# Neighbour tables as one stream of slots with masked steps, and TensorE sums four rows of each step of the last attention

## The chip, the cores and the metric

One Trainium2 chip, one core. The metric is the device time of one execution in microseconds, the median of three: 5052.19 us before the change (5048.85 to 5056.97).

## The reference, cut to what matters

A network of four graph layers and four expert layers on 3125 nodes of 256 features. Two of its layers are attentions over in-edges with a softmax per target node: the gate of layer 1 (65536 edges of which those with both ends among the nodes count, 4 heads of 4 features) and the last graph layer (100000 edges, 8 heads of 32 features). The last one, which the change touches most:

```python
def _L3_gnn_ref(x, edge_index, W, att_src, att_dst, bias):
    h = jnp.einsum('nf,fhd->nhd', x, W)
    a_src = jnp.sum(h * att_src, axis=-1)
    a_dst = jnp.sum(h * att_dst, axis=-1)
    e = jax.nn.leaky_relu(a_src[src] + a_dst[dst], NEG_SLOPE)
    e_max = jax.ops.segment_max(e, dst, num_segments=N)
    e_exp = jnp.exp(e - e_max[dst])
    denom = jax.ops.segment_sum(e_exp, dst, num_segments=N)
    alpha = e_exp / (denom[dst] + 1e-16)
    msg = h[src] * alpha[:, :, None]
    out = jax.ops.segment_sum(msg, dst, num_segments=N)
    out = out.reshape(N, -1) + bias
    return jax.nn.relu(out)
```

It is followed by eight gelu experts of which each node takes two.

## The kernel before

**Tiles and stages.** The nodes are sorted by in-degree and lie in 25 tiles of 128, one node per partition; a tile needs as many slots as its largest in-degree. These are for the main graph 55, 42, 40, 39, 38, 37, 36, 35, 34, 34, 33, 32, 32, 31, 31, 30, 30, 29, 28, 28, 27, 26, 25, 23, 20 (together 815), for the gate's graph 28, 19, 17, 16, 16, 15, 15, 14, 14, 13, 13, 13, 12, 12, 11, 11, 11, 10, 10, 9, 9, 9, 8, 7, 5. The stages follow one another: "graphs" builds the tables of neighbours, "count" and the following ones (l0p, l0a, l0f, l0e) do layer 0, l1a is the gate's attention beside the experts of layer 1, l2a and l2e are layer 2, l3p prepares the rows and l3a is the last attention beside its experts.

**The tables.** In build_graphs, `fill` (L638) has VectorE lay out each tile's neighbours in the tile `ell`, 64 slots a node, and SyncE (even tiles, L338) and ScalarE's queue (odd ones, L261) write them to HBM by `write_tile` (L234): a block of 128 x 8 numbers for the main graph, 128 x 4 for the gate's, one DMA each (L239). Each tile starts at a block of its own, so its slots are rounded up: 112 blocks of 8, 92 blocks of 4. The values of empty slots (8191) are outside of the rows and gather nothing. `steps_of` (L680) plans for the gate's graph how many blocks of a tile are taken alone and how many in pairs. VectorE's last work in the stage is to place the weights of layer 2 (L3103).

**The last attention** (attend_heads_beside_experts, L2228). One step takes 8 slots. SyncE loads their indices into one of four buffers (L2338 to L2339), POOL gathers 8 rows of 264 numbers each with one indirect DMA per slot (L2355), waiting first that VectorE is done with the buffer, and VectorE does the rest in `edges` (L2508): scores (L2514), a refill of the buffer's scores with -1e30 for gathers that will skip slots (L2515), leaky relu (L2516), running maximum (L2517), difference (L2518), and a copy (L2520); ScalarE does the exp into PSUM (L2379). Before VectorE waits for that it runs `add_sums` (L2533) for the previous step's rows: 8 weighted rows to 4, 2, 1 and onto the accumulator (L2536 to L2539). After the wait it scales the accumulator (L2526), copies the weights as a 33rd column (L2527) and multiplies the 8 rows with them (L2528). A tile is an opening step, half of the pieces of expert work that fall to this tile (`at(0)`), the later steps in a loop, the other half (`at(1)`), the closing sums, and the division.

**The order of the work** is written out by hand in `tiles` (L2277): every engine runs through the same list, four tiles of attention to each group of four tiles of expert work, two pieces a tile. In one piece TensorE makes one expert's products (L2449) and the one before's outputs (L2459), ScalarE the gelus (L2393), and VectorE adds an earlier expert's output onto x (L2638). TensorE has nothing to do with the attention's steps, and after the last tile it runs the rest of the last group's experts.

**The gate's attention** (attend_beside_experts, L2660) is built alike, with rows of 24 numbers and buffers of two units of 4 slots; a step takes one unit or two, and VectorE works on each unit by its own instruction (L2936, L2949). Five registers are loaded for each tile. Between tiles stand the pieces of layer 1's experts (L2780, L2791). There are 34 steps of one unit and 29 of two.

`ch(...)` issues an instruction and waits for its end; `ch.add(...)` issues without waiting, and `ch.join()` waits for all of them.

## Time and profile before

| | us |
|---|---|
| median of three | 5052.19 |
| the profiled execution | 5050.65 |
| its span | 5049.0 |
| PE busy | 2837.1 |
| DVE (VectorE) busy | 3175.9 |
| ACT (ScalarE) busy | 1613.8 |
| POOL (GpSimd) busy | 2036.4 |

The mean granted TensorE clock is 0.83 of 2.4 GHz. The busy times don't add up to the span, since the engines work beside each other; no engine is busy throughout, so what bounds the kernel differs by stage and has to be read from stretches and waits.

### The profile page before, as it was taken

The page shows a single profiled execution, that of the slowest core. Times are in us where ns is not written, and L with a number is a line of the kernel's source. Part 1 is how long each engine was busy: PE and PEld are TensorE (multiplying, and loading weights), DVE is VectorE, ACT ScalarE, POOL GpSimd, SP SyncE. Part 2 cuts the span into 40 slices and gives each one's busy share as a digit, 9 for nine tenths or more (in the row PEclk, how much of TensorE's full clock was granted, in tenths as well). Part 3 has the DMA queues.
Part 4 walks back from the last instruction along what each step waited for, and adds up shares of the span by engine and source line. Part 5 has one row for each costly group of instructions (what it writes and reads, how often), then busy time and mean ns, then how long its engine had stood idle before and what let it go on. Part 6 is the DMA issues. An engine that isn't in the chain of part 4 may idle for free. (4 is left out here: it accounts for less than half of the span.)

```text
span 5049.0 us, 66259 instructions
## 1 busy us (share of the span) xinstructions
PE 2837.1 (56%) x15435; PEld 2098.0 (42%) x15474; DVE 3175.9 (63%) x7737; ACT 1613.8 (32%) x2880; POOL 2036.4 (40%) x1967
## 2 busy tenths in 40 slices
PE   0541055699799596467761699859400133344447
PEld 0431055587687485355551244447300122222224
DVE  8886687677577656334436754452456777777774
ACT  0243043476476121144430454322201222222222
POOL 1136410200100152577761100016377777777771
PEclk9999999899899598588885899979755566667679
DMA  0412345542442323211114554522343333333220
GB/s 33 77 20 45 17 167 196 170 139 83 166 140 83 116 65 115 91 30 35 35 38 132 196 174 161 172 91 67 101 117 91 90 90 85 93 95 84 77 63 19
DMA packets 341260, 487.28 MB, mean 97 GB/s; under 512 B 171624, under 2 KB 259056, under 8 KB 339059
## 3 DMA queue, kind: packets, MB, share of 16 engines
q1 hardware_dynamic: 204434, 259.76, 16.5%
q0 software_dynamic: 86064, 176.05, 13.2%
q10 hardware_dynamic: 50608, 49.90, 3.0%
q14 instruction: 116, 0.94, 0.1%
q8 instruction: 38, 0.62, 0.1%
HBM read 369.96 MB, written 137.24 MB: 100 GB/s over the span
## 5 line engine op out<-in xcount | busy, mean ns | idle before, releaser
L2355 POOL DMA_INDIRECT l3a_got<-rows,l3a_idx x896 | 949.4, 1060 | 304.1 <-issue 273.6
L2449 PE MATMUL ps<-l3a_xt,l3a_w 128*128 128x512 f32 (+1 forms) x448 | 266.9, 759 | 633.1 <-ACT l3a_h L2393 633.1
L1662 PE MATMUL ps<-l0a_all_rows,l0a_w 128*128 128x257 f32 x2500 | 556.8, 382 | 28.3 <-DVE l0a_w L1782 28.3
L1662 PEld LDWEIGHTS ps<-l0a_all_rows,l0a_w 128*128 128x128 f32 x2500 | 476.0, 191 | 101.9 <-issue 32.0
L2757 POOL DMA_INDIRECT l1a_got<-rows,l1a_idx x384 | 383.6, 999 | 131.3 <-issue 127.4
L2449 PEld LDWEIGHTS ps<-l3a_xt,l3a_w 128*128 128x128 f32 x448 | 112.3, 277 | 766.9 <-issue 766.6
L2077 PE MATMUL ps<-l2a_table,l2a_count 128*128 128x512 bf16 x1837 | 404.8, 380 | 40.5 <-ACT l2a_count L2002 38.6
L2379 ACT ACT_TABLE_LOAD x99 | 127.0, 1283 | 772.0 <-DVEq L2519 772.0
L2780 PE MATMUL ps<-xt,l1w_w 128*128 x640 | 208.0, 485 | 156.5 <-ACT l1a_h L2836 111.4
L2077 PEld LDWEIGHTS ps<-l2a_table,l2a_count 128*128 128x128 bf16 x1875 | 183.4, 98 | 262.1 <-issue 43.2
L1587 ACT ACTIVATE l0a_low<-ps,l0a_factors x650 | 254.6, 510 | 85.7 <-PE ps L1652 78.2
L2528 DVE TENSOR_TENSOR l3a_v<-l3a_got,ps 128x2048 f32<-128x2048 f32 x112 | 255.0, 2276 | 0.0
L3338 POOL DMA_INDIRECT l0e_xin<-routed,l0e_taking x60 | 64.0, 1067 | 450.5 <-DVEq L3534 424.0
L2459 PE MATMUL ps<-l3a_w,l3a_h 128*128 128x256 f32 x800 | 199.8, 405 | 81.5 <-DVEq L2641 79.8
L2780 PEld LDWEIGHTS ps<-xt,l1w_w 128*128 128x128 f32 x640 | 135.2, 214 | 225.9 <-issue 181.6
L2459 PEld LDWEIGHTS ps<-l3a_w,l3a_h 128*128 128x128 f32 x800 | 160.9, 204 | 129.4 <-issue 108.1
L1166 POOL DMA_INDIRECT rows<-own_rows,node x50 | 48.9, 977 | 403.8 <-DVEq L1034 394.0
L1782 DVE TENSOR_TENSOR l0a_w<-l0a_w,l0a_held 128x1280 f32<-128x1280 f32 x130 | 192.7, 1484 | 13.2 <-DVE xt L1817 13.2
L2791 PE MATMUL ps<-l1w_w,l1a_h 128*128 128x256 f32 x800 | 180.5, 385 | 29.9 <-ACT l1a_h L2836 29.9
L2791 PEld LDWEIGHTS ps<-l1w_w,l1a_h 128*128 128x128 f32 x800 | 154.5, 194 | 52.6 <-issue 31.0
L1973 POOL DMA_DIRECT2D l2a_seen<-l2a_state x13 | 9.2, 704 | 410.6 <-DMA l2a_state<-l2a_seen 385.7
L1768 DVE TENSOR_TENSOR l0a_w<-l0a_w,l0a_low 128x1280 f32<-128x1280 f32 x78 | 116.4, 1493 | 82.2 <-ACT l0a_w L1593 71.9
(995 smaller groups left out, 6622.9 us busy)
## 6 DMA issues: line engine op xcount, KB each, us to landing
l0a_held<-counts SPq DMA_DIRECT2D x130, 640.0 KB, 3.9
counts<-count_held SPq DMA_DIRECT2D x13, 3200.0 KB, 9.9
l2a_held<-counts SPq DMA_DIRECT2D x65, 640.0 KB, 4.0
l3a_got<-rows,l3a_idx POOLq DMA_INDIRECT x896, 2.8
l_y<-l1a_y_sb ACTq DMA_DIRECT2D x20, 640.0 KB, 3.4
l2a_table<-rows SPq DMA_DIRECT2D x16, 640.0 KB, 7.5
l2a_state<-l1a_fresh ACTq DMA_DIRECT2D x1, 9984.0 KB
l2a_seen<-l2a_state POOLq DMA_DIRECT2D x12, 768.0 KB, 5.9
```

What stands on the lines that cost most here:

```text
L1587: ins = act.activation(low_at(n * Q + q, h), spread_of(n, W, 2 * W), ACT.Copy, scale=factors[:, C, at:at + 1])
L1662: ins = pe.matmul(sums_of(n, k, D + 1), w[:, at, k * P:(k + 1) * P], all_rows[:, at, 1:RW], start=(at == 0), stop=False)
L1782: dve.tensor_tensor(chunk(q), chunk(q), held_of(n, q), ALU.mult).then_inc(weighed, 1)
L2077: ins = pe.matmul(bank_of(b, g, k).rearrange("p o n -> p (o n)"), count[:, at, k * P:(k + 1) * P], table[:, part, at, :], start=(at == 0 a ...
L2355: pool.indirect_dma_start(out=got[:, at:at + RW], out_offset=None, in_=rows[:, :], in_offset=bass.IndirectOffsetOnAxis(ap=idx[:, a, k:k + ...
L2379: act.activation(p, d[:, :, :], ACT.Exp).then_inc(exped, 1)
L2449: ins = pe.matmul(ps[:, m, 0:size * P], w1[:, x, k, m * P:(m + 1) * P], xt[:, 0:size, k, :], start=(k == 0), stop=(k == KT - 1))
L2459: ins = pe.matmul(ps[:, 2 + j // 2, (j % 2) * D:(j % 2 + 1) * D], h[:, x % 2, m, j * P:(j + 1) * P], w2[:, x, m, :], start=(m == 0), stop= ...
L2528: ch.add(dve.tensor_tensor(rows_v[:, :, :, 0:DH], buffer(b)[:, :, 0:D].rearrange("p s (h d) -> p s h d", h=H), p[:, 0:SLOTS, :].unsqueeze( ...
L2757: pool.indirect_dma_start(out=got[:, at:at + RW], out_offset=None, in_=rows[:, :], in_offset=bass.IndirectOffsetOnAxis(ap=idx[:, a, k:k + ...
L2780: ins = pe.matmul(ps[:, 2 * (m % 2) + q, 0:(hi - lo) * P], w1[:, x, k, m * P:(m + 1) * P], xt[:, bass.ds(i * C + lo, hi - lo), k, :], star ...
L2791: ins = pe.matmul(ps[:, 4 + j // 2, (j % 2) * D:(j % 2 + 1) * D], h[:, m, j * P:(j + 1) * P], w2[:, x, m, :], start=(m == 0 and j % 2 == 0 ...
```

## The change

The tables become [128, columns], one stream of slots: each tile gets as many slots as its largest in-degree (at least 8), and the next tile's follow at once. A step still takes 8 slots that begin at a multiple of 8, so that a tile can share its first and its last octet with its neighbours; a mask of -1e30 is added to the scores of the slots that belong to others. Empty slots point to a row behind the last node's, which SyncE writes before the gathers, so buffers are not refilled. SyncE and ScalarE's queue write only full octets of a tile, wait for all of them, and then write one closing octet per tile that may overlap the one before. In the last attention VectorE adds four of the eight weighted rows onto the others, and TensorE sums the four into a PSUM bank with products with the identity; VectorE adds this onto the accumulator one step later. The counting stage fetches a tile's slots as one run per partition. In l2a a constant and a shift change with the table's unit.

The diff, cut to its core:

```diff
-UNIT = 4
+FEWEST = SLOTS
...
-def write_tile(eng, s, t, stored):
-    n_units = eng.value_load(s.trips_i[0:1, bass.ds(t, 1)], min_val=1, max_val=s.whole_row)
-    to = eng.value_load(s.dest_i[0:1, bass.ds(t, 1)], min_val=0, max_val=s.blocks - s.whole_row)
-    with eng.Fori(0, n_units) as u:
-        eng.dma_start(s.table[bass.ds((to + u) * (P * s.slots), P * s.slots), 0].rearrange("(p s) -> p s", s=s.slots),
-                      s.ell[:, bass.ds(t, 1), bass.ds(u * s.slots, s.slots)].rearrange("p o s -> p (o s)")).then_inc(stored, 16)
+def write_table(eng, s, odd, emptied=None):
+    eng.wait_ge(s.sized, 1)
+    n = eng.value_load(s.chunk_i[0:1, 0:1], min_val=1, max_val=s.chunks)
+    with eng.Fori(0, n) as k:
+        for half, (lo, hi) in enumerate(s.halves):
+            when(eng, c, s.filled, k * 2 + (half + 1))
+            with eng.Fori((lo + 1 - odd) // 2, (hi + 1 - odd) // 2) as h:
+                t = h * 2 + odd
+                n_units = eng.value_load(s.trips_i[0:1, bass.ds(t, 1)], min_val=1, max_val=s.whole_row)
+                to = eng.value_load(s.dest_i[0:1, bass.ds(t, 1)], min_val=0, max_val=s.columns - WIDE)
+                with eng.Fori(0, n_units) as u:
+                    eng.dma_start(s.table[:, bass.ds(to + u * SLOTS, SLOTS)],
+                                  s.ell[:, bass.ds(t, 1), bass.ds(SLOTS + u * SLOTS, SLOTS)].rearrange("p o s -> p (o s)")).then_inc(s.stored, 16)
+        done = eng.value_load(s.wrote_i[0:1, 0:1], min_val=1, max_val=s.chunks * NT * s.whole_row)
+        when(eng, c, s.stored, done * 16)
+        with eng.Fori(0, (NT + 1 - odd) // 2) as h:
+            t = h * 2 + odd
+            at = eng.value_load(s.last_i[0:1, 0, bass.ds(t, 1)], min_val=1, max_val=WIDE)
+            to = eng.value_load(s.last_i[0:1, 1, bass.ds(t, 1)], min_val=0, max_val=s.columns - WIDE)
+            eng.dma_start(s.table[:, bass.ds(to, SLOTS)],
+                          s.ell[:, bass.ds(t, 1), bass.ds(at, SLOTS)].rearrange("p o s -> p (o s)")).then_inc(s.closed, 16)
+        if emptied is not None:
+            when(eng, c, s.closed, k * (16 * NT) + 16 * NT)
+            eng.sem_inc(emptied, 1)
...
+def whole_table(s):
+    write_table(sp, s, 0, s.emptied)
+    total = sp.value_load(s.base_row[0:1, NT:NT + 1], min_val=1, max_val=s.trash - 2 * WIDE)
     for k in range(2):
-        sp.dma_start(s.table[bass.ds((total + k * s.whole_row) * (P * s.slots), P * WIDE), 0].rearrange("(p s) -> p s", s=WIDE),
-                     empty[:, :]).then_inc(s.padded, 16)
-even_tiles(m)
-even_tiles(g)
+        sp.dma_start(s.table[:, bass.ds(total + k * WIDE, WIDE)], empty[:, :]).then_inc(s.padded, 16)
+whole_table(m)
+whole_table(g)
...
-ch(dve.tensor_scalar(units[:, 0:NT], row[:, 0:NT], float(s.slots * (s.least - 1) + 1), float(s.slots - 1), ALU.max, ALU.add))
-ch(dve.tensor_copy(row_i[:, 0:NT], units[:, 0:NT]))
-ch(dve.tensor_scalar(row_i[:, 0:NT], row_i[:, 0:NT], s.slots.bit_length() - 1, None, ALU.logical_shift_right))
-ch(dve.tensor_copy(units[:, 0:NT], row_i[:, 0:NT]))
+ch(dve.tensor_scalar(units[:, 0:NT], row[:, 0:NT], float(FEWEST), None, ALU.max))
...
-m.ch.add(dve.memset(empty[:, :], NOBODY))
+m.ch.add(dve.memset(empty[:, :], c.N))
...
-steps_of(g, True)
...
-b = eng.value_load(base_row[0:1, bass.ds(i * 2 + par, 1)], min_val=0, max_val=blocks - 2 * UNITS)
-at = (b + k * UNITS) % units
-eng.dma_start(tile[:, par, :].rearrange("p (u s) -> p u s", s=SLOTS),
-              table[bass.ds(at * (P * SLOTS), P * WIDE), 0].rearrange("(u p s) -> p u s", p=P, s=SLOTS)).then_inc(landed, 16)
+b = eng.value_load(base_row[0:1, bass.ds(i * 2 + par, 1)], min_val=0, max_val=columns - 2 * WIDE)
+at = (b + k * WIDE) % total
+eng.dma_start(tile[:, par, :], table[:, bass.ds(at, WIDE)]).then_inc(landed, 16)
...
+class Stream:
+    def __init__(self, c, table, base_row):
+        self.base_row, self.columns = base_row, table.shape[1]
+        self.table, self.NT = table, c.NT
+    def total(self, eng):
+        return eng.value_load(self.base_row[0:1, self.NT:self.NT + 1], min_val=1, max_val=self.columns - 4 * WIDE)
+    def rounds(self, total):
+        return (total + RING * SLOTS) // (RING * SLOTS)
+    def octet(self, o):
+        return self.table[:, bass.ds(o * SLOTS, SLOTS)]
+    def bounds(self, eng, t):
+        begins = eng.value_load(self.base_row[0:1, bass.ds(t, 1)], min_val=0, max_val=self.columns - 4 * WIDE)
+        ends = eng.value_load(self.base_row[0:1, bass.ds(t + 1, 1)], min_val=FEWEST, max_val=self.columns - 4 * WIDE)
+        return begins, ends
+def fill_masks(dve, ch, c, masks):
+    row = c.iota[:, 0:SLOTS].unsqueeze(2).broadcast_to([P, SLOTS, SLOTS])
+    slot = c.iota[:, 0:SLOTS].unsqueeze(1).broadcast_to([P, SLOTS, SLOTS])
+    ch.add(dve.tensor_tensor(masks[:, 0, :, :], slot, row, ALU.is_lt))
+    ch.add(dve.tensor_tensor(masks[:, 1, :, :], slot, row, ALU.is_ge))
+    ch.add(dve.memset(masks[:, 2, :, :], 0.0))
+    ch.join()
+    ch(dve.tensor_scalar(masks[:, 0:2, :, :], masks[:, 0:2, :, :], FLOOR, None, ALU.mult))
+def mask_of(masks, row, H):
+    return masks[:, :, :, :].rearrange("p k r j -> p (k r j)")[:, bass.ds(row * SLOTS, SLOTS)].unsqueeze(2).broadcast_to([P, SLOTS, H])
+def closing_row(ends, o):
+    return SLOTS + ends % SLOTS + (ends // SLOTS - o + 65535) // 65536 * SLOTS
...
+weighed_rows = lambda o: rows_v[:, bass.ds(o % 2, 1), :, :, :].rearrange("p o s h d -> p (o s) h d")
+totals = ps[:, 6, 0:VW]
...
+sp.wait_ge(blank, 2)
+sp.dma_start(rows[c.N:c.N + 1, :], nobody[:, :]).then_inc(blank_in, 16)
...
-total = pool.value_load(base_row[0:1, c.NT:c.NT + 1], min_val=1, max_val=blocks - 2 * RING)
-last_node = pool.to_reg(c.N - 1)
-with pool.Fori(0, (total + (RING - 1)) // RING) as q:
+rounds = stream.rounds(stream.total(pool))
+last_node, last_row = pool.to_reg(c.N - 1), pool.to_reg(c.N)
+pool.wait_ge(blank_in, 16)
+with pool.Fori(0, rounds) as q:
     for a in range(RING):
         when(pool, c, idx_in[a], (q + 1) * 16)
-        when(pool, c, valued, q * (2 * RING) + (2 * a + 2))
+        when(pool, c, freed, q * RING + (a + 1))
...
+def sums(t, o):
+    when(pe, c, valued, o + t + 1)
+    rows_now = weighed_rows(o)
+    for k in range(ADDED):
+        ins = pe.matmul(totals, c.ident[:, :], rows_now[:, k, :, :].rearrange("p h d -> p (h d)"),
+                        start=(k == 0), stop=(k == ADDED - 1))
+    ins.then_inc(summed, 1)
+def tile(t, begins, ends, at):
+    sums(t, begins // SLOTS)
     at(0)
+    with pe.Fori(begins // SLOTS + 1, ends // SLOTS + 1) as o:
+        sums(t, o)
...
-    ch(dve.memset(buffer(a), FLOOR))
-    dve.sem_inc(valued, 2)
+dve.memset(nobody[:, 0:D], 0.0).then_inc(blank, 1)
+dve.memset(nobody[:, D:RW], FLOOR).then_inc(blank, 1)
+dve.sem_inc(freed, RING)
+fill_masks(dve, ch, c, masks)
...
-def edges(t, b, opening):
+def edges(t, o, row, opening):
     ch.restart()
-    when(dve, c, arrived, b + 1)
-    scores = buffer(b)[:, :, D:RW]
+    when(dve, c, arrived, o + 1)
+    rows_now = weighed_rows(o)
     er = c.er[:, bass.ds(t * 8, H)].unsqueeze(1).broadcast_to([P, SLOTS, H])
-    ch(dve.tensor_tensor(e[:, 0:SLOTS, :], scores, er, ALU.add))
-    ch.add(dve.tensor_scalar(scores, e[:, 0:SLOTS, :], 0.0, FLOOR, ALU.mult, ALU.add))
+    ch(dve.tensor_tensor(e[:, 0:SLOTS, :], buffer(o)[:, :, D:RW], er, ALU.add))
+    ch(dve.tensor_tensor(e[:, 0:SLOTS, :], e[:, 0:SLOTS, :], mask_of(masks, row, H), ALU.add))
     ch(dve.scalar_tensor_tensor(e[:, 0:SLOTS, :], e[:, 0:SLOTS, :], SLOPE, e[:, 0:SLOTS, :], ALU.mult, ALU.max))
     ch(dve.tensor_reduce(top[:, :], e[:, :, :].rearrange("p s h -> p h s"), AX, ALU.max))
     ch(dve.tensor_tensor(d[:, :, :], e[:, :, :], top[:, :].unsqueeze(1).broadcast_to([P, SLOTS + 1, H]), ALU.subtract))
     dve.sem_inc(shifted, 1)
     ch.add(dve.tensor_copy(e[:, SLOTS, :], top[:, :]))
-    if not opening:
-        add_sums()
     dve.wait_ge(exped, 1)
     dve.sem_clear(exped)
-    ch.add(dve.tensor_tensor(acc[:, :, :], acc[:, :, :], spread(p[:, SLOTS, :], DH + 1), ALU.mult))
-    ch.add(dve.tensor_copy(rows_v[:, :, :, DH], p[:, 0:SLOTS, :]))
-    ch.add(dve.tensor_tensor(rows_v[:, :, :, 0:DH], buffer(b)[:, :, 0:D].rearrange("p s (h d) -> p s h d", h=H),
+    ch.add(dve.tensor_copy(rows_now[:, :, :, DH], p[:, 0:SLOTS, :]))
+    ch.add(dve.tensor_tensor(rows_now[:, :, :, 0:DH], buffer(o)[:, :, 0:D].rearrange("p s (h d) -> p s h d", h=H),
                              p[:, 0:SLOTS, :].unsqueeze(3).broadcast_to([P, SLOTS, H, DH]), ALU.mult))
     ch.join()
-    dve.sem_inc(valued, 2)
-def add_sums():
-    rows = rows_v
-    ch(dve.tensor_tensor(rows[:, 0:4, :, :], rows[:, 0:4, :, :], rows[:, 4:8, :, :], ALU.add))
-    ch(dve.tensor_tensor(rows[:, 0:2, :, :], rows[:, 0:2, :, :], rows[:, 2:4, :, :], ALU.add))
-    ch(dve.tensor_tensor(rows[:, 0, :, :], rows[:, 0, :, :], rows[:, 1, :, :], ALU.add))
-    ch(dve.tensor_tensor(acc[:, :, :], rows[:, 0, :, :], acc[:, :, :], ALU.add))
-def tile(t, b0, b1, at):
+    ch(dve.tensor_tensor(rows_now[:, 0:ADDED, :, :], rows_now[:, 0:ADDED, :, :], rows_now[:, ADDED:SLOTS, :, :], ALU.add))
+    if not opening:
+        add_sums(o + t)
+        ch(dve.tensor_tensor(acc[:, :, :], acc[:, :, :], spread(p[:, SLOTS, :], DH + 1), ALU.mult))
+    dve.sem_inc(valued, 1)
+def add_sums(done):
+    when(dve, c, summed, done)
+    ch(dve.tensor_tensor(acc[:, :, :], by_head(totals), acc[:, :, :], ALU.add))
+def tile(t, begins, ends, at):
     ch.restart()
     ch.add(dve.memset(e[:, SLOTS, :], START))
     ch.add(dve.memset(acc[:, :, :], 0.0))
     ch.join()
-    edges(t, b0, True)
+    edges(t, begins // SLOTS, begins % SLOTS, True)
     at(0)
-    with dve.Fori(b0 + 1, b1) as b:
-        edges(t, b, False)
+    with dve.Fori(begins // SLOTS + 1, ends // SLOTS + 1) as o:
+        dve.sem_inc(freed, 1)
+        edges(t, o, closing_row(ends, o), False)
     ch.restart()
     at(1)
-    add_sums()
+    add_sums(ends // SLOTS + t + 1)
...
-def bounds_of(eng, t):
-    b0 = eng.value_load(step_rows[0:1, 0, bass.ds(t, 1)], min_val=0, max_val=blocks)
-    alone = eng.value_load(step_rows[0:1, 1, bass.ds(t, 1)], min_val=1, max_val=2)
-    pairs = eng.value_load(step_rows[0:1, 2, bass.ds(t, 1)], min_val=1, max_val=blocks)
-    return b0, alone, pairs
...
-when(pool, c, freed, q * (2 * RING) + (2 * a + 2))
+when(pool, c, freed, q * RING + (a + 1))
...
-def edges(b, unit, lo):
+def edges(o, row):
     ch.restart()
-    parts = [(unit + h, lo + h * UNIT) for h in range((SLOTS - lo) // UNIT)]
-    here, through, last = slice(lo, SLOTS), slice(lo, SLOTS + 1), len(parts)
-    when(dve, c, arrived, unit + last)
-    er = er_of.broadcast_to([P, UNIT, H])
-    for u, at in parts:
-        ch.add(dve.tensor_tensor(e[:, at:at + UNIT, :], buffer(u, VW, VW + H), er, ALU.add))
-    ch.join()
-    for u, at in parts:
-        ch.add(dve.tensor_scalar(buffer(u, VW, VW + H), er, 0.0, FLOOR, ALU.mult, ALU.add))
-    ch(dve.scalar_tensor_tensor(e[:, here, :], e[:, here, :], SLOPE, e[:, here, :], ALU.mult, ALU.max))
-    ch(dve.tensor_reduce(top[:, :], e[:, through, :].rearrange("p s h -> p h s"), AX, ALU.max))
-    ch(dve.tensor_tensor(d[:, through, :], e[:, through, :], top[:, :].unsqueeze(1).broadcast_to([P, SLOTS + 1 - lo, H]), ALU.subtract))
+    when(dve, c, arrived, o + 1)
+    ch(dve.tensor_tensor(e[:, 0:SLOTS, :], buffer(o, VW, VW + H), er_of.broadcast_to([P, SLOTS, H]), ALU.add))
+    ch(dve.tensor_tensor(e[:, 0:SLOTS, :], e[:, 0:SLOTS, :], mask_of(masks, row, H), ALU.add))
+    ch(dve.scalar_tensor_tensor(e[:, 0:SLOTS, :], e[:, 0:SLOTS, :], SLOPE, e[:, 0:SLOTS, :], ALU.mult, ALU.max))
+    ch(dve.tensor_reduce(top[:, :], e[:, :, :].rearrange("p s h -> p h s"), AX, ALU.max))
+    ch(dve.tensor_tensor(d[:, :, :], e[:, :, :], top[:, :].unsqueeze(1).broadcast_to([P, SLOTS + 1, H]), ALU.subtract))
     dve.sem_inc(shifted, 1)
     ch(dve.tensor_copy(e[:, SLOTS, :], top[:, :]))
     dve.wait_ge(weighed, 1)
     dve.sem_clear(weighed)
-    for u, at in parts:
-        ch.add(dve.tensor_tensor(
-            v[:, at:at + UNIT, :].rearrange("p s (h d) -> p s h d", h=H),
-            buffer(u, 0, VW).rearrange("p s (h d) -> p s h d", h=H),
-            p[:, at:at + UNIT, :].unsqueeze(3).broadcast_to([P, UNIT, H, DH]), ALU.mult))
+    ch.add(dve.tensor_tensor(v[:, :, :].rearrange("p s (h d) -> p s h d", h=H),
+                             buffer(o, 0, VW).rearrange("p s (h d) -> p s h d", h=H),
+                             p[:, 0:SLOTS, :].unsqueeze(3).broadcast_to([P, SLOTS, H, DH]), ALU.mult))
     ch.add(dve.tensor_tensor(by_head(acc), by_head(acc), spread(p[:, SLOTS, :]), ALU.mult))
     ch.join()
-    dve.sem_inc(freed, last)
     ch.add(dve.tensor_tensor(p[:, SLOTS, :], p[:, SLOTS, :], den, ALU.mult))
-    ch.add(dve.tensor_reduce(part[:, :], v[:, here, :].rearrange("p s w -> p w s"), AX, ALU.add))
+    ch.add(dve.tensor_reduce(part[:, :], v[:, :, :].rearrange("p s w -> p w s"), AX, ALU.add))
     ch.join()
-    ch.add(dve.tensor_reduce(den, p[:, through, :].rearrange("p s h -> p h s"), AX, ALU.add))
+    ch.add(dve.tensor_reduce(den, p[:, :, :].rearrange("p s h -> p h s"), AX, ALU.add))
     ch.add(dve.tensor_tensor(acc, acc, part[:, :], ALU.add))
     ch.join()
-b0, alone, pairs = bounds_of(dve, t)
-u0 = dve.value_load(base_row[0:1, bass.ds(t, 1)], min_val=0, max_val=blocks)
-u1 = dve.value_load(step_rows[0:1, 3, bass.ds(t, 1)], min_val=1, max_val=blocks)
-with dve.Fori(0, alone) as i:
-    edges(b0 + i, u0 + i, UNIT)
+begins, ends = stream.bounds(dve, t)
+edges(begins // SLOTS, begins % SLOTS)
 beside()
-with dve.Fori(0, pairs) as i:
-    edges(b0 + alone + i, u1 + i * 2, 0)
+with dve.Fori(begins // SLOTS + 1, ends // SLOTS + 1) as o:
+    dve.sem_inc(freed, 1)
+    edges(o, closing_row(ends, o))
```

## Rows read from the trace of the kernel before

**Rows 1.** Gathers of both attentions; first and last step of l3a.
```profile
L2355 POOL DMA_INDIRECT l3a_got<-rows,l3a_idx x896 | 949.4, 1060 | 304.1 <-issue 273.6
...
L2757 POOL DMA_INDIRECT l1a_got<-rows,l1a_idx x384 | 383.6, 999 | 131.3 <-issue 127.4
...
L2514 DVE TENSOR_TENSOR l3a_e<-l3a_got,er x112: 224/226/269, 3691.0 to 4932.8; 128x64 f32 x64, 128x64 f32<-128x64 f32 x48
```

**Rows 2.** Busy time by stretches: span, PE, PEld, DVE, ACT, POOL, PEclk, DMA share, GB/s.
```profile
3690.00:3790.00 100.00, 0.00 (x0) 0.00 (x0) 69.65 (x143) 7.03 (x15) 77.76 (x74) 0.50 0.33 84
...
4800.00:4900.00 100.00, 40.34 (x124) 25.14 (x124) 76.83 (x175) 23.54 (x31) 69.52 (x66) 0.73 0.25 64
```

**Rows 3.** Waits of stage l3a: total us, times, longest.
```profile
DVE l3a_e L2514 <- SPq L2338: 87.1, 27, 16.2
...
POOL l3a_got L2355 <- DVEq L2531: 22.8, 8, 5.4
```

**Rows 4.** VectorE in order of time: start, length, operation, [idle before].
```profile
4598.71 0.22 DVE L2514 TENSOR_TENSOR l3a_e<-l3a_got,er 128x64 f32 x1 [0.59 <-DVE l3a_acc L2544]
...
4600.14 0.17 DVE L2520 COPY l3a_e<-l3a_top 128x8 f32<-128x8 f32 x1
...
4601.81 0.43 DVE L2526 TENSOR_TENSOR l3a_acc<-l3a_acc,ps 128x264 f32<-128x264 f32 x1 [1.50 <-ACT ps L2379]
...
4605.17 1.66 DVE L2638 SCALAR_TENSOR_TENSOR x<-ps,l3a_g_now,x 128x256 f32 x4 [0.60 <-DVE l3a_v L2528]
...
4618.11 0.23 DVE L2514 TENSOR_TENSOR l3a_e<-l3a_got,er 128x64 f32 x1 [0.94 <-DVE l3a_v L2528]
...
4618.37 0.19 DVE L2515 TENSOR_SCALAR l3a_got<-l3a_e 128x64 f32 x1
...
4618.48 0.22 DVE L2516 SCALAR_TENSOR_TENSOR l3a_e<-l3a_e 128x64 f32<-128x64 f32 x1
...
4619.43 0.17 DVE L2520 COPY l3a_e<-l3a_top 128x8 f32<-128x8 f32 x1
...
4622.57 0.43 DVE L2526 TENSOR_TENSOR l3a_acc<-l3a_acc,ps 128x264 f32<-128x264 f32 x1
...
4626.25 0.23 DVE L2514 TENSOR_TENSOR l3a_e<-l3a_got,er 128x64 f32 x1 [0.92 <-DVE l3a_v L2528]
```

**Rows 5.** ScalarE, TensorE in order of time; then the table loads of l3a.
```profile
4600.15 1.28 ACT L2379 ACT_TABLE_LOAD   x1 [17.88 <-DVEq L2519]
...
4601.44 0.23 ACT L2379 ACTIVATE ps<-l3a_d 128x72 f32<-128x72 f32 x1
...
4603.82 5.15 PE L2449 MATMUL ps<-l3a_xt,l3a_w 128*128 128x512 f32 x8 [11.76 <-ACT l3a_h L2393]
...
4608.81 3.62 PE L2459 MATMUL ps<-l3a_w,l3a_h 128*128 128x256 f32 x16
...
L2379 ACT ACT_TABLE_LOAD x99 | 127.0, 1283 | 772.0 <-DVEq L2519 772.0
```

**Rows 6.** Busy time by stretches of l1a, columns as in rows 2.
```profile
2300.00:2400.00 100.00, 73.03 (x275) 55.81 (x276) 40.73 (x219) 39.97 (x63) 76.53 (x78) 0.85 0.17 35
...
2500.00:2600.00 100.00, 87.43 (x355) 67.43 (x354) 39.87 (x207) 45.87 (x72) 75.95 (x77) 0.95 0.18 39
```

**Rows 7.** VectorE by line, 4300 to 4957: busy us, mean ns | idle before.
```profile
L2536 DVE TENSOR_TENSOR l3a_v<-l3a_v 128x1056 f32<-128x1056 f32 x56 | 70.2, 1254 | 1.9
```

**Rows 8.** Waits of stage l1a.
```profile
DVE l1a_e L2936 <- DMA l0a_held<-counts: 91.2, 21, 5.0
```

**Rows 9.** SyncE's queue and VectorE at the end of the graphs stage.
```profile
466.31 79.27 SPq L239 DMA_DIRECT2D table_main<-graphs_main_ell  x59
...
556.01 0.88 SPq L351 DMA_DIRECT2D table_main<-graphs_empty  x2
...
559.58 66.92 SPq L239 DMA_DIRECT2D table_gate<-graphs_five  x49
...
634.73 1.89 DVE L3103 COPY_PREDICATED wt<-graphs_set_mask,graphs_set_w_now 128x256 f32<-128x256 int32 x4
```

245 lines of the change are left out of this document (108 added, 137 removed).

## The prediction

> **What bounds the kernel now.** I read the busy table by stretches first, then the waits, then single steps in order of time. The steps of the last attention (stage l3a) run from 3691.0 to 4932.8 us on VectorE [rows 1]. Early on POOL is busy 77.8 us of 100 and VectorE 69.7; near the end POOL has fallen to 69.5 and VectorE risen to 76.8 [rows 2]. One gather of the gate attention takes 1.00 us busy with 0.33 us of issue around it [rows 1], and those here mostly the same, so 77% is about all that POOL can show: the first part goes by gathers, and the later part by VectorE. The waits agree: VectorE waits 87.1 us for gathered octets, POOL only 22.8 us for freed buffers [rows 3]. So VectorE has 87 us of slack in the whole stage; whatever it gains or loses beyond that is the stage's time, since the TensorE tail starts from its last tile.
>
> A later step of VectorE takes 8.14 us, 4618.11 to 4626.25 [rows 4]. Of these the exp wait is fully hidden: ACT's exp needs a 1.28 us table load and 0.23 us [rows 5], and in that time VectorE does the four sums of the step before, 3.14 us from the copy (4619.43) to the scaling (4622.57). The opening step has no sums to do and shows the bare wait: copy 4600.14, scaling 4601.81, 1.67 us with 1.50 of it idle for ACT; it takes 6.46 us up to the work after it at 4605.17 [rows 4]. The gate attention (l1a) is bound by gathers: POOL 76 to 77% busy in every stretch [rows 6], and of its 131.3 us idle all but 3.9 is issue [rows 1].
>
> **The change, part by part.** *Counts.* From the in-degrees of the 25 tiles (55, 42, 40, ... 20; sum 815 slots), the main table had 112 octets, so 112 steps and 896 gathers. As a stream it has 815 slots, 104 octets with the last round, 832 gathers; but a tile that begins and ends inside octets touches more of them: 126 steps, 25 opening and 101 later ones instead of 87. The gate table (321 slots) goes from 384 to 352 gathers, and from 63 steps (34 of half width) to 65 of full width.
>
> *A later step of l3a.* From 8.14: take out the stretch of the sums, -3.14, and put in the bare exp wait, +1.67. The refill of the buffer goes, -0.11 (4618.37 to 4618.48, where the next operation begins beside it). A mask add of the size of the first add comes in, chained, +0.26 (4618.11 to 4618.37). The scaling of the accumulator leaves its old place, -0.35, and stands at the end behind a chain, +0.46. The first of the old adds, 1056 elements, 1.254 us [rows 7], stays but no longer covers anything, +1.28 with its gap. Adding TensorE's totals from PSUM, 264 elements: +0.55 with the wait. Sum 8.76 us. *Opening step:* 6.46 - 0.11 + 0.26 - 0.35 + 1.28 = 7.54. *Closing:* the four sums, 3.0 us, become one add, 0.55. Together: 101 x 8.76 - 87 x 8.14 = +177; 25 x 1.08 = +27; -25 x 2.45 = -61. That is **+142 us** of VectorE's own time: fewer elements per step, but more steps, and the cover of exp gone.
>
> *Registers.* The mask's row, the octet's parity and two buffer addresses are computed by VectorE's sequencer. Part runs under the operation before. Nothing shows this arithmetic; bounds 0 (all hidden) and 0.7 us a step (nearly the 0.92 us by which 4626.25 follows one step's product [rows 4], again), 0 to +88; I take 0.2 us, **+25**, since most of it can be done before the operation it waits for ends.
>
> *Waiting for TensorE.* Each step gives TensorE four fp32 products with the identity, 264 columns, 8 records. The 16 records of 256 columns took 3.62 us [rows 5], so 1.87 us at that pace. TensorE will have been idle for some microseconds before; where it is idle the granted clock is 0.50 [rows 2], the 1.2 GHz level, so twice that, 3.7 us. In later steps it is hidden (the totals are wanted a whole step later). At a tile's close the experts' adds take 1.7 to 1.9 us, 4605.17 for four [rows 4], and the rest shows: 25 x 1.8 = **+45** (0 at the 2.4 GHz level).
>
> *Slack.* VectorE's 87.1 us of waiting for octets goes, since POOL now needs 832 x 1.31 = 1090 us, the 1.31 being 1.00 / 0.767 [rows 6], against VectorE's nearly 1400: **-87** (-60 if part of it is the first tiles waiting behind SP's weight loads). POOL's waits for freed buffers grow instead and cost nothing.
>
> So l3a: +142 + 25 + 45 - 87 = **+125**.
>
> *Gate attention.* 32 gathers fewer at 1.33 us [rows 1] is -42. VectorE loses three of five register loads per tile (the 91.2 us idle before its first add, 21 times 4.3 us [rows 8], labelled with a DMA it doesn't wait for), and gains a mask add and wider steps; it has room, being about 40% busy. In the late tiles TensorE is 87% busy [rows 6] and keeps the pace, so part is lost there: **-35** (-50 to -25). POOL's wait for SP's write of the empty row is 2 to 3 us at the start, within this.
>
> *Building the tables.* SP writes 59 units of the main table in 79.3 us and 49 of the gate's in 66.9 [rows 9], and ACT the rest beside it. It now writes only full units (90 of 112, and about 31 of 92, over both queues), then waits for all to land (10.4 us passed from the last issue to the pad at 556.01; with fewer writes I take 7 to landing), then writes one closing octet per tile, 13 on SP at about 2.3 us with their two register loads (a fit to the two SP rows: 1.0 us within a tile, 2.55 across). Main: 536, landed 543, closed 575. Gate: full ones by 614, closed by 647, padded by 652. VectorE's last placing ends at 636.6 [rows 9], and this is what ends the stage now: **+15** (0 to +35). The step plan that goes (2.6 us) and the small operations that come into the fill cancel.
>
> The counting's fetch of one run of 256 bytes a partition in place of eight short ones: the fetches run a pair of tiles ahead of their use, and only the first, one short transfer, is waited for; 0. Changes in l2a are one constant and a shift; 0.
>
> **Sum:** +125 - 35 + 15 = +105 on the profiled execution's own 5050.65 us (span 5049.0), which is 1.5 below the median of the three: **5155 us**.
>
> **A rule against the trace.** The exp begins at 4601.44 where the load of 4600.15 ends: a switch costs 1.28 us, and the bare wait is 1.50 [rows 4, 5]. The Trainium skill ("ScalarE: Activation LUTs", "What ACT_TABLE_LOAD costs") adds a drain of about 1.38 us to each switch; the trace has none in this chain. If it showed up once the wait is exposed, 126 steps would lose about 174 us more, an estimate from that page's figure, and the time would be about 5330.
>
> **Rivals.** (1) *Gathers stay the bound, faster.* l3a would shrink by 64 x 1.33 = 85, l1a by 42, building +15: 4939 us. For it: POOL at 77% [rows 2]. Against: it holds only while VectorE needs less than 10.5 us per gathered octet, and I get (1242 - 87 + 212) / 104, 13.1: the stage's steps without their waits, and what is added. 0.05. (2) *Exp without its table load.* 99 of the 112 exps had one; without them 126 x 1.28 = 161 less: 4994. For it: in most later steps exp follows exp, with no other function between. Against: if all 25 opening steps have a load, 74 of the 87 later ones have one too [rows 5], so they are loaded again regardless. 0.04. (3) *Hidden after all.* Registers, closing wait and building at 0: 142 - 87 - 35 = +20, 5071. 0.12. (4) *TensorE in lockstep is late.* Behind each opening step it has an expert turn, 5.15 + 3.62 us [rows 5], before the next step's sums; at the 1.2 GHz level about 17 us against VectorE's 18.6 until it needs them. If it misses by 3 us a tile, +75: 5230. 0.08. (5) The drain, 5330: 0.02. (6) The counts aren't what I say: 0.01, any side. The forecast keeps 0.68.
>
> **Numbers.** A measurement of this kernel tells about 0.2% (10 us) from no change. Forecast with its bounds (registers -25 to +63, closing wait -45 to 0, slack 0 to +27, building -15 to +20, l1a -15 to +10), not all at one end: 5095 to 5210; the range reaches down to rival 3 and up to rival 4. Faster: rivals 1, 2 and a tail of 3, 0.10. Same: 0.06. Slower: 0.84.
>
> **What would show it.** Right: 126 scores, 832 and 352 gathers; after the copy of each later step VectorE idle about 1.5 us for ACT; later steps 8.9 to 9.0 us apart; POOL's idle put down to VectorE freeing buffers; VectorE no longer waiting for SP; the counting stage begun at about 652. Wrong: a later step under 8.3 us, exp without its load, POOL still 77% busy throughout, or VectorE waiting for TensorE's sums inside a tile.

## The result, and the profile after

The changed kernel takes 5318.77 us (5317.60 to 5319.46, 4 runs) against 5053.5 of the kernel before in the same comparison: a ratio of 1.0525, 95% interval 1.0507 to 1.0544. It is slower, as forecast, but by 265 us where 105 were forecast, and outside of the range of 5070 to 5230. The profiled execution took 5319.1 us, 268.5 more than that of before.

Lines of the page after: the span, the busy times, the granted clock by slices, and the costliest groups that answer to those of before.

```profile
span 5317.5 us, 69508 instructions
...
PE 3201.6 (60%) x16481; PEld 2369.6 (45%) x16482; DVE 3158.9 (59%) x7592; ACT 1635.9 (31%) x2910; POOL 1951.8 (37%) x1871
...
PEclk9999999899997896798858998896666677677778
...
L2384 POOL DMA_INDIRECT l3a_got<-rows,l3a_idx x832 | 909.6, 1093 | 607.7 <-DVEq L2587 350.4
...
L2455 PE MATMUL ps<-l3a_v,ident 128*128 x1008 | 446.2, 618 | 767.8 <-DVEq L2573 767.8
...
L2408 ACT ACT_TABLE_LOAD x112 | 143.7, 1283 | 970.8 <-DVEq L2560 970.8
```

The counts are those of the forecast: 832 gathers, 126 steps (1008 records of TensorE's sums are 126 times 8). VectorE's busy time fell, from 3175.9 to 3158.9 us, while the kernel grew by 5%: the time is not in the operations but between them. The stretches of the last attention, early and late, in the columns of [rows 2]:

```profile
3710.00:3810.00 100.00, 34.23 (x72) 22.59 (x72) 59.04 (x114) 6.39 (x14) 77.73 (x74) 0.59 0.46 100
4800.00:4900.00 100.00, 56.90 (x168) 39.51 (x168) 62.82 (x134) 21.14 (x28) 60.31 (x55) 0.72 0.27 73
```

POOL begins at its 77% and ends at 60, and VectorE is at 63% where it was at 77: nobody is busy, so something waits. The waits of the stage (total us, times, longest):

```profile
DVE l3a_v L2565 <- ACT ps L2408: 192.5, 125, 2.0
...
DVE l3a_e L2556 <- DVE l3a_e L2555: 67.5, 126, 0.7
...
DVE l3a_e L2555 <- SPq L2366: 29.6, 4, 18.2
...
DVE l3a_acc L2578 <- PE ps L2455: 22.9, 11, 4.4
...
POOL l3a_got L2384 <- DVEq L2587: 350.4, 23, 21.2
```

VectorE stands 192.5 us for the exp (34.3 in the 24 opening steps before), and 67.5 us between its first two operations. Its wait for gathers fell from 87.1 [rows 3] to 29.6 us, and POOL now waits 350.4 us for VectorE to free buffers. Where the waits lie in a step is seen in order of time (start, length, operation, [idle before]); this is the later step that answers to the 8.14 us of [rows 4]:

```profile
4702.30 0.23 DVE L2555 TENSOR_TENSOR l3a_e<-l3a_got,er 128x64 f32 x1 [0.98 <-DVE l3a_acc L2572]
...
4703.13 0.23 DVE L2556 TENSOR_TENSOR l3a_e<-l3a_e,l3a_masks 128x64 f32<-128x64 f32 x1 [0.60 <-DVE l3a_e L2555]
...
4704.37 0.17 DVE L2561 COPY l3a_e<-l3a_top 128x8 f32<-128x8 f32 x1
...
4706.21 0.27 DVE L2565 COPY l3a_v<-ps 128x64 f32 x1 [1.67 <-ACT ps L2408]
...
4706.37 2.29 DVE L2566 TENSOR_TENSOR l3a_v<-l3a_got,ps 128x2048 f32 x1
...
4708.82 1.26 DVE L2569 TENSOR_TENSOR l3a_v<-l3a_v  x1 [0.16 <-DVE l3a_v L2566]
...
4710.32 0.43 DVE L2578 TENSOR_TENSOR l3a_acc<-ps,l3a_acc 128x264 f32<-128x264 f32 x1 [0.24 <-DVE l3a_v L2569]
...
4710.78 0.43 DVE L2572 TENSOR_TENSOR l3a_acc<-l3a_acc,ps 128x264 f32<-128x264 f32 x1
...
4712.18 0.22 DVE L2555 TENSOR_TENSOR l3a_e<-l3a_got,er 128x64 f32 x1 [0.97 <-DVE l3a_acc L2572]
```

From 4702.30 to 4712.18 it takes 9.88 us. ScalarE in the same step:

```profile
4704.38 1.28 ACT L2408 ACT_TABLE_LOAD   x1 [8.37 <-DVEq L2560]
4705.68 0.23 ACT L2408 ACTIVATE ps<-l3a_d 128x72 f32<-128x72 f32 x1
```

Between the first add (L2555) and the mask (L2556) VectorE stands 0.60 us. The view by line gives what its queue does there; under it are the same two operations in an opening step, whose mask row is `begins % SLOTS` and needs less arithmetic than `closing_row`:

```profile
L2556 DVEq FUSED_REGOPS  x227: 113/176/322, 3711.4 to 5195.7; - x114
...
4730.51 0.23 DVE L2555 TENSOR_TENSOR l3a_e<-l3a_got,er 128x64 f32 x1 [0.67 <-DVE l3a_acc L2583]
...
4730.93 0.23 DVE L2556 TENSOR_TENSOR l3a_e<-l3a_e,l3a_masks 128x64 f32<-128x64 f32 x1 [0.20 <-DVE l3a_e L2555]
```

FUSED_REGOPS are register operations (count, then shortest, median and longest in ns). In the later step above they run from 4702.56 to 4703.08: they begin 0.04 us after the first add has ended, and so they do in the other steps (median of 126). `ch(...)` has VectorE's queue wait for the end of an operation before it takes the next thing in the program, and the arithmetic stands behind that wait. Nothing covers it.

The time of the whole, by the first and last operation of the stages on VectorE, in the profiled executions: the counting begins at 654.8 instead of 638.4 us (+16.4); the stages up to the gate's attention add 5.4; the gate's attention with what waits for it, from its first operation to the gate's own, takes 556.7 instead of 560.5 (-3.8); up to the first score of the last attention +2.1; from the first to the last step's score there 1484.0 instead of 1241.8 (+242.2); the rest +6.2. Sum +268.5.

### The profile page after: what moved, and what is told of

Read it like the earlier page. It is cut to its first block and busy times, and to the rows that moved or that the text cites. A ratio compares the mean times of both kernels' runs of the same rounds, so it can differ in the third digit from the quotient of the medians.

```text
span 5317.5 us, 69508 instructions
## 1 busy us (share of the span) xinstructions
PE 3201.6 (60%) x16481; PEld 2369.6 (45%) x16482; DVE 3158.9 (59%) x7592; ACT 1635.9 (31%) x2910; POOL 1951.8 (37%) x1871
## 5 line engine op out<-in xcount | busy, mean ns | idle before, releaser
L2384 POOL DMA_INDIRECT l3a_got<-rows,l3a_idx x832 | 909.6, 1093 | 607.7 <-DVEq L2587 350.4
L2455 PE MATMUL ps<-l3a_v,ident 128*128 x1008 | 446.2, 618 | 767.8 <-DVEq L2573 767.8
L2455 PEld LDWEIGHTS ps<-l3a_v,ident 128*128 128x128 f32 x1008 | 297.4, 309 | 904.2 <-issue 834.1
L2794 POOL DMA_INDIRECT l1a_got<-rows,l1a_idx x352 | 351.1, 997 | 158.7 <-issue 117.4
L2566 DVE TENSOR_TENSOR l3a_v<-l3a_got,ps 128x2048 f32 x126 | 288.4, 2289 | 1.0 <-issue 1.0
L2489 PE MATMUL ps<-l3a_xt,l3a_w 128*128 128x512 f32 (+1 forms) x448 | 200.7, 596 | 8.6 <-ACT l3a_h L2422 8.5
L2499 PE MATMUL ps<-l3a_w,l3a_h 128*128 128x256 f32 x800 | 187.4, 387 | 3.5 <-DVEq L2681 3.5
L2569 DVE TENSOR_TENSOR l3a_v<-l3a_v x126 | 158.6, 1259 | 19.8 <-DVE l3a_v L2566 19.8
```

Of the source, the lines that this page charges most:

```text
L2384: pool.indirect_dma_start(out=got[:, at:at + RW], out_offset=None, in_=rows[:, :], in_offset=bass.IndirectOffsetOnAxis(ap=idx[:, a, k:k + ...
L2455: ins = pe.matmul(totals, c.ident[:, :], rows_now[:, k, :, :].rearrange("p h d -> p (h d)"), start=(k == 0), stop=(k == ADDED - 1))
L2489: ins = pe.matmul(ps[:, m, 0:size * P], w1[:, x, k, m * P:(m + 1) * P], xt[:, 0:size, k, :], start=(k == 0), stop=(k == KT - 1))
L2499: ins = pe.matmul(ps[:, 2 + j // 2, (j % 2) * D:(j % 2 + 1) * D], h[:, x % 2, m, j * P:(j + 1) * P], w2[:, x, m, :], start=(m == 0), stop= ...
L2566: ch.add(dve.tensor_tensor(rows_now[:, :, :, 0:DH], buffer(o)[:, :, 0:D].rearrange("p s (h d) -> p s h d", h=H), p[:, 0:SLOTS, :].unsqueez ...
L2569: ch(dve.tensor_tensor(rows_now[:, 0:ADDED, :, :], rows_now[:, 0:ADDED, :, :], rows_now[:, ADDED:SLOTS, :, :], ALU.add))
```

## Experiments

The theory I tested: VectorE's own chain of dependent operations sets the last attention, and the step grew by the bare wait for the exp, by the mask, and by register arithmetic between the operations. The rivals: TensorE in lockstep sets the pace; or the stream's additional steps alone cost nearly everything. The kernel before took 5051 to 5056 us beside all runs but three, which are named. The diffs are in the last attention, unless it says otherwise.

**blocks_pe_sums: TensorE's sums alone, with the tables of before.**

```diff
-                    if not opening:
-                        add_sums()
                     dve.wait_ge(exped, 1)
...
                     dve.sem_inc(valued, 2)
+                    halve(b)
+                    if not opening:
+                        add_sums(b)
+                        ch(dve.tensor_tensor(acc[:, :, :], acc[:, :, :], spread(p[:, SLOTS, :], DH + 1), ALU.mult))
+                    dve.sem_inc(halved, 1)
```

> The kernel before with its tables as they are, and only the sums of the last attention moved: VectorE adds four of eight rows after the product, TensorE sums the four. The chain theory (VectorE's own chain of dependent operations with the bare exp wait in it sets l3a): a later step goes from 8.14 to about 9.2 us, the closing sums shrink; own time +70 us, of which the 87 us in which VectorE waited for gathers take in a part: 5065 to 5125 us, likeliest 5090. The rival that TensorE's products are what is waited for: most of the change's 265 us is here too, 5200 or more.

Measured 5098.87 us, ratio 1.0086 (1.0056 to 1.0115). A later step takes 9.10 us (median), 0.96 more than before. The two waits that tell it:

```profile
DVE l3a_v L2539 <- ACT ps L2382: 169.1, 111, 2.0
...
DVE l3a_e L2529 <- SPq L2341: 43.2, 13, 16.6
```

The exp's wait is there in all steps, and half of VectorE's 87.1 us of waiting for gathers has been used up to pay for it. So moving the sums costs 43 us by itself.

**stream_own_sums: the stream and its masks alone,** with the sums back on VectorE in the exp wait.

```diff
                     ch.add(dve.tensor_copy(e[:, SLOTS, :], top[:, :]))
+                    if not opening:
+                        add_sums()
                     dve.wait_ge(exped, 1)
...
-                    ch(dve.tensor_tensor(rows_now[:, 0:ADDED, :, :], rows_now[:, 0:ADDED, :, :], rows_now[:, ADDED:SLOTS, :, :], ALU.add))
-                    if not opening:
-                        add_sums(o + t)
```

> The changed kernel with its stream of slots and its masks, but with the sums of the last attention done by VectorE in the exp wait, as before. The chain theory: a later step at 8.9 to 9.1 us (8.14, less the refill, plus 0.83 for the mask and its row), 101 of them: 5200 to 5230 us. If the 14 more steps and the mask cost little: under 5120.

Measured 5220.26 us, ratio 1.0326 (1.0296 to 1.0356); a later step 8.84 us, slightly under what was expected, the whole inside. The stream is the larger part, +164 us; it and the sums make 207 of the 265. Most of the missing 58 is slack that can be spent only once: of VectorE's 87.1 us of waiting for gathers 43.2 are left in blocks_pe_sums, 31.3 here and 29.6 in the change, so the two halves took 43.9 and 55.8 and the whole only 57.5, which is 42 less. Another 13 are 14 more steps with the 0.96 us of blocks_pe_sums.

**middle_unmasked: masks only on a tile's first and last octet.**

```diff
-                    with dve.Fori(begins // SLOTS + 1, ends // SLOTS + 1) as o:
+                    with dve.Fori(begins // SLOTS + 1, ends // SLOTS) as o:
                         dve.sem_inc(freed, 1)
-                        edges(t, o, closing_row(ends, o), False)
+                        edges(t, o, None, False)
+                    dve.sem_inc(freed, 1)
+                    edges(t, ends // SLOTS, ends % SLOTS + SLOTS, False)
```

> The changed kernel, with the loop over later steps ended one octet earlier and without mask, and the closing octet written out behind it with its mask; the result is the same, since only a tile's first and last octet hold slots of others. The chain theory: 76 of 101 later steps lose the mask add and the arithmetic on its row, 0.83 us each, and the closing one some of the arithmetic: -63 to -75 us, 5244 to 5256. If the row's arithmetic is hidden or something else bounds the steps: less than -30 us.

Measured 5249.92 us, ratio to before 1.0384 (1.0354 to 1.0415), 69 us under the change. An operation of 0.23 us and the register arithmetic for its row in each of the 76 middle steps, 0.91 us a step, cost a quarter of the whole loss, and they are not needed there: only first and last octets hold slots of other tiles.

**one_product: one of TensorE's four products in each step** (three of the four rows are left out of the sums).

```diff
-                    for k in range(ADDED):
+                    for k in range(1):
```

> The changed kernel, but TensorE forms only one of the four products of each step (it leaves out three of the four rows from the sums). The chain theory: nothing inside a tile waits for TensorE, only the closings do (about 2 us in some tiles): -10 to -35 us, 5285 to 5309. The rival that TensorE in lockstep sets the pace: -100 us or more.

Measured 5302.43 us (5296.68 to 5308.17), -16; with two runs 11 us apart that is a rough figure. With a quarter of the products the step still takes 9.88 us, and VectorE's wait for TensorE's sums falls from 22.9 us in 11 waits to 2.5 in 2. TensorE in lockstep does not set the pace; it is waited for at closings only.

**blocks_bare_exp: the kernel before, with its sums behind the exp's wait instead of ahead of it.**

```diff
-                    if not opening:
-                        add_sums()
-
                     dve.wait_ge(exped, 1)
                     dve.sem_clear(exped)
+                    if not opening:
+                        add_sums()
```

> The kernel before with one thing changed: in the last attention VectorE waits for the exp first and sums the previous step's rows only then. The chain theory: a later step goes from 8.14 to 9.8 us (the bare wait of 1.84 in place of the 0.17 of the copy), 87 of them, +145 us of own time, less the 60 to 87 us that VectorE waited for gathers: 5115 to 5170. If the exp's cover is worth little: under 5085.

Measured 5152.07 us, ratio 1.0192 (1.0172 to 1.0212): the order of four lines is worth 96 us, with no operation added. A later step takes 9.74 us, and VectorE waits 150 us for the exp in the stage. The wait in one step, from the copy to the first of the sums:

```profile
4625.69 0.27 DVE L2520 COPY l3a_e<-l3a_top 128x8 f32<-128x8 f32 x1
...
4627.37 1.26 DVE L2536 TENSOR_TENSOR l3a_v<-l3a_v 128x1056 f32<-128x1056 f32 x1 [1.40 <-ACT ps L2379]
```

The step is 1.6 us longer, the length of the wait (1.68), and not by the 3.14 us of the sums: about half of the sums was covered, the other half VectorE paid already before.

**late_row_add: the change, with the add of four rows moved into the next step's exp wait.**

```diff
                     ch.add(dve.tensor_copy(e[:, SLOTS, :], top[:, :]))
+                    if not opening:
+                        halve(o + 1)
                     dve.wait_ge(exped, 1)
...
-                    ch(dve.tensor_tensor(rows_now[:, 0:ADDED, :, :], rows_now[:, 0:ADDED, :, :], rows_now[:, ADDED:SLOTS, :, :], ALU.add))
                     if not opening:
                         add_sums(o + t)
...
+                    halve(ends // SLOTS)
                     at(1)
                     add_sums(ends // SLOTS + t + 1)
```

On TensorE a tile's first sum moves with it, behind the first half of the expert work.

> The changed kernel with the add of four rows onto four moved from behind the product into the next step's exp wait, so TensorE gets them one step later. The chain theory: the 1.50 us of the add leave the chain, but VectorE now waits for TensorE's totals of the previous step: handed over 1.3 us into the exp wait, 3.88 us of products at the 1.2 GHz level, against the product's end 4.4 us after the copy: about 1.1 us of new wait, none at the 2.4 GHz level. So 9.4 us a later step, -35 to -50 us: 5265 to 5285; with TensorE at the upper level -110: 5210. If VectorE's sequencer rather than the chain sets the pace: no gain.

Measured 5336.57 us (5334.63 to 5338.50): 18 slower than the change, a miss. A later step takes 9.82 us (median), as good as unchanged. VectorE and, in the last row, TensorE in one step:

```profile
4706.83 1.31 DVE L2577 TENSOR_TENSOR l3a_v<-l3a_v  x1
...
4708.54 0.27 DVE L2566 COPY l3a_v<-ps 128x64 f32 x1 [0.41 <-ACT ps L2408]
...
4708.69 2.29 DVE L2567 TENSOR_TENSOR l3a_v<-l3a_got,ps 128x2048 f32 x1
...
4712.57 0.43 DVE L2583 TENSOR_TENSOR l3a_acc<-ps,l3a_acc 128x264 f32<-128x264 f32 x1 [1.58 <-PE ps L2455]
...
4708.53 3.88 PE L2455 MATMUL ps<-l3a_v,ident 128*128 x8 [6.05 <-DVEq L2578]
```

The add (4706.83) is indeed out of the chain. But TensorE gets its rows only at 4708.5 and takes 3.88 us; VectorE's product ends at 4710.98, and it stands until 4712.57. What the add gave, TensorE's products took. I had estimated 1.1 us for this wait, with the rows handed over 1.3 us behind the copy of 4706.53; they were handed over 2.0 us behind it, because 0.30 us pass before the add begins and 0.39 between its end (4708.14) and the first product. Where the 18 us come from is not shown: they are not in the later steps.

**late_one_product: the same with one product,** which leaves out three of four rows of the sums.

```diff
-                    for k in range(ADDED):
+                    for k in range(1):
```

> The kernel of late_row_add (the add of four rows in the next step's exp wait) with one of TensorE's four products in each step (three of four rows are left out of the sums). If late_row_add gained nothing because VectorE waits 1.58 us a step for TensorE's slow products, this wait goes: 9.82 to 8.3 to 8.6 us a later step, 5336 to 5185 to 5220. If something else took the place of the add (the sequencer, the exp), it stays over 5300.

In that comparison the kernel before itself took 5424 us (5404 to 5447) and this one 5408.4, so that neither can be set against other runs. The same holds for the first runs of stream_own_unmasked and blocks_empty_row. All three kernels were run again.

> The same kernel as late_one_product, again, for the same reason. If late_row_add gained nothing because VectorE waits 1.58 us a step for TensorE: 8.3 to 8.6 us a later step (it had 8.48 there), 5185 to 5220. If something else took the add's place: over 5300.

Measured 5196.90 us (5194.96 to 5198.83), 140 under late_row_add, as expected. VectorE's product and its next operation, and TensorE:

```profile
4715.39 2.29 DVE L2567 TENSOR_TENSOR l3a_v<-l3a_got,ps 128x2048 f32 x1
...
4717.92 0.43 DVE L2583 TENSOR_TENSOR l3a_acc<-ps,l3a_acc 128x264 f32<-128x264 f32 x1 [0.25 <-DVE l3a_v L2567]
...
4715.23 0.71 PE L2455 MATMUL ps<-l3a_v,ident 128*128 x2 [1.21 <-DVEq L2578]
```

With about 1 us of products the add follows the product by 0.25 us, and a later step takes 8.47 us (median), 1.41 less than in the change. So the wait of late_row_add was TensorE's, and without it the exp covers nearly all of the add's 1.50 us. This kernel leaves out three quarters of the sums; it shows what the cover is worth, not a way to have it.

**blocks_late_two_rows: an attempt at a kernel better than both.** The tables of before; VectorE adds 8 rows to 4 and to 2 in the exp wait, TensorE sums the two.

```diff
+                def halve(b):
+                    last = weighed_rows(b)
+                    ch(dve.tensor_tensor(last[:, 0:4, :, :], last[:, 0:4, :, :], last[:, 4:8, :, :], ALU.add))
+                    ch(dve.tensor_tensor(last[:, 0:2, :, :], last[:, 0:2, :, :], last[:, 2:4, :, :], ALU.add))
+                    dve.sem_inc(halved, 1)
```

> The tables of before; VectorE adds 8 rows to 4 and to 2 in the exp wait of the next step (1.25 and 0.71 us), TensorE sums the two, and VectorE adds the total onto the accumulator behind the product. The chain theory: exp stays covered, TensorE's four records (1.9 us at the 1.2 GHz level) are done before they are wanted; 8.14 - 3.14 - 0.35 + 2.2 + 0.95 = 7.8 us a later step, and the closing sums shorter by 1: own time -30 to -50 us, of which gathers take back part: 5015 to 5050, faster than both kernels. If TensorE's totals come late: 5060 or more.

Measured 5106.44 us (5101.74 to 5107.75), ratio 1.0103 (1.0086 to 1.0119): a miss, 50 slower than before.

```profile
4607.57 1.26 DVE L2552 TENSOR_TENSOR l3a_v<-l3a_v  x1
...
4608.98 0.71 DVE L2553 TENSOR_TENSOR l3a_v<-l3a_v  x1 [0.16 <-DVE l3a_v L2552]
...
4610.09 0.27 DVE L2540 COPY l3a_v<-ps 128x64 f32 x1 [0.40 <-ACT ps L2382]
...
4612.79 0.43 DVE L2559 TENSOR_TENSOR l3a_acc<-ps,l3a_acc 128x264 f32<-128x264 f32 x1 [0.26 <-DVE l3a_v L2541]
...
4610.09 2.12 PE L2429 MATMUL ps<-l3a_v,ident 128*128 x4 [6.40 <-DVEq L2554]
```

A later step takes 8.62 us (median), not 7.8. From the copy of the maximum (4607.29) to the copy of the weights (4610.09) 2.80 us pass, where 2.2 were counted: 0.28 pass ahead of the first add, and after the second add VectorE stands 0.40 us more. The profile puts that down to ScalarE, but the exp, begun at 4608.60, took 0.23 us and was long over. The records of VectorE's queue fill the 0.40: the signal to TensorE at 4609.73, the clearing of the exp's semaphore at 4609.84, the address arithmetic of the copy at 4609.93, the copy at 4610.09. TensorE, in the last row, begins at the same moment. The same 0.41 stands in late_row_add, where the exp was over too. So a hand-over and an address between two dependent operations cost 0.4 us where 0.1 had stood (0.14 from the sums' end to the scaling in the kernel before). No division of the sums that I tried beat all four adds in the exp wait.

**gate_ring_six: six buffers in the gate's attention of the changed kernel.**

```diff
+    SIX = 6
...
-        idx = sb("idx", [P, RING, SLOTS], I32)
-        got = sb("got", [P, RING * SLOTS * RW])
+        idx = sb("idx", [P, SIX, SLOTS], I32)
+        got = sb("got", [P, SIX * SLOTS * RW])
```

> The changed kernel with six instead of four buffers in the gate's attention, so also 336 in place of 352 gathers (its last round is less empty). Theory of late buffers: an octet that two tiles share is freed only in the second tile's first later step, POOL waits 41 us for buffers and this is what the stage lost: POOL's wait goes, l1a 15 to 30 us shorter, 5288 to 5303. The rival that the late tiles go at the pace of TensorE's expert turns and of VectorE's longer steps: 0 to -8 us, 5310 to 5319.

Measured 5306.65 us (5306.56 to 5306.75), -12, between the two theories, and the trace shows where they lie. In the change: POOL waits for buffers; VectorE has the attention's last result at 2630.72, POOL issues its last gather at 2634.09, and SyncE writes out the result at 2641.18.

```profile
POOL l1a_got L2794 <- DVEq L2996: 41.3, 19, 6.2
...
2630.55 0.17 DVE L3003 TENSOR_TENSOR l1a_found<-l1a_both,l1a_bias 128x16 f32<-128x16 f32 x1
...
2634.09 1.00 POOL L2794 DMA_INDIRECT l1a_got<-rows,l1a_idx  x1 [0.30 <-issue]
...
2641.18 0.38 SPq L2780 DMA_DIRECT2D l1a_by_gate<-l1a_found  x1
```

With six buffers POOL waits 4.8 us in all, VectorE's result comes at the same time, and it is written at once:

```profile
2630.33 0.17 DVE L3004 TENSOR_TENSOR l1a_found<-l1a_both,l1a_bias 128x16 f32<-128x16 f32 x1
...
2630.62 0.38 SPq L2781 DMA_DIRECT2D l1a_by_gate<-l1a_found  x1
```

The last tile begins at 2616.6 and 2616.5 us, and all but the first tile and the fourth (2.3 and 1.1 us) begin within 0.8 us of one another; the attention itself is no faster. The 10.6 us lie behind it. SyncE comes to the write only after it has waited for every gather of the last round, and in the change that round ends with octets that no tile needs, gathered late because their buffers came free late. Six buffers need 336 gathers instead of 352, and the last of them is issued long before; in the kernel before, too, the write followed VectorE's result at once (2625.77 and 2625.89). So the surplus gathers of the last round cost 10.6 us once, at the end. The run changes both the number of buffers and the number of gathers and doesn't divide the two. The tiles before go on at their pace: VectorE's steps and TensorE's turns are left as what sets it, and no run here divides these.

**stream_own_unmasked: the stream, VectorE's own sums in the exp wait, and masks only where they are needed.** Its edits are those of stream_own_sums and middle_unmasked together:

```diff
+                    if not opening:
+                        add_sums()
...
-                        edges(t, o, closing_row(ends, o), False)
+                        edges(t, o, None, False)
```

> The stream of slots with VectorE's own sums in the exp wait (as stream_own_sums) and masks only on a tile's first and last octet (as middle_unmasked). What is left over the kernel before is then the 14 more steps, the closing of the tables and the gate's attention. The chain theory: a middle step at 8.05 us, -65 us from 5220: 5150 to 5162. If VectorE comes so close to the gathers that POOL sets the pace again: over 5170.

> The same kernel as stream_own_unmasked, again, for the same reason. The chain theory: a middle step at 8.05 us (8.07 there), 5150 to 5162; if POOL sets the pace again: over 5170.

In the disturbed comparison 5402.61 us beside 5424.15; run again, 5151.31 (5148.38 to 5154.24), ratio 1.0200 (1.0180 to 1.0221). The copy, and the operation behind the four sums (3.14 us, as in [rows 4]):

```profile
4703.72 0.27 DVE L2551 COPY l3a_e<-l3a_top 128x8 f32<-128x8 f32 x1
...
4706.86 0.43 DVE L2557 TENSOR_TENSOR l3a_acc<-l3a_acc,ps 128x264 f32<-128x264 f32 x1
```

A middle step takes 8.09 us, what it took before. With the step as short as ever the stream still costs 100 us. In the profiled execution the first score of the last attention comes 20 us later than in the kernel before, and from there to the last step's score it takes 80 us more (1321.9 instead of 1241.8): 14 more steps of 8.1 us are 113, less 38 us of the waiting for gathers (87.1 became 49.1).

**blocks_empty_row: the row for empty slots alone,** in the kernel before.

```diff
-                for a in range(RING):
-                    ch(dve.memset(buffer(a), FLOOR))
+                dve.memset(nobody[:, 0:D], 0.0).then_inc(blank, 1)
+                dve.memset(nobody[:, D:RW], FLOOR).then_inc(blank, 1)
...
-                    ch.add(dve.tensor_scalar(scores, e[:, 0:SLOTS, :], 0.0, FLOOR, ALU.mult, ALU.add))
```

> The kernel before with the empty row alone in the last attention: empty slots point to a row behind the last node's, SyncE writes it before the gathers, and VectorE neither fills the buffers at the start nor refills them in each step. The chain theory: 0.11 us a step, 12 us of VectorE's own time, and part of it hidden where gathers set the pace: -3 to -12 us, 5043 to 5053, the only part of the change that would make the kernel faster. If writing the row delays the first gathers: 0 to +5.

> The same kernel as blocks_empty_row, again, because the kernel before took 5424 us beside it instead of 5054 and neither could be compared with the other runs. As there: 0.11 us a step, 12 us of VectorE's own time, part of it hidden: -3 to -12 us against before. If writing the row delays the first gathers: 0 to +5.

In the disturbed comparison 5455.34 us beside 5424.15; run again in 10 runs, 5049.24 us, ratio 0.9995 (0.9985 to 1.0004): no difference that can be told, though a later step became 0.08 us shorter (8.16 to 8.08, medians of the steps without a wait for gathers).

## Why the prediction was wrong

The direction was right, and so was what bounds the last attention: VectorE's chain with the bare exp wait in it. The size was not. Of the 163.5 us between the forecast of +105 and the +268.5 of the profiled executions, 117 lie in the last attention, 31 in the gate's, 1 in the tables, and 14 in stages that the forecast put at 0 (5.4, 2.1 and 6.2; what they are was not looked into).

**Registers: the step that failed.** The forecast bounded the arithmetic by 0 and 0.7 us a step and took 0.2; measured about 1.1, the whole difference between the forecast chain (8.76) and the step (9.88). By the rows of a later step: from the first add to the mask 0.83 us where 0.26 was forecast (+0.57); from the copy of the maximum to that of the weights 1.84 against 1.67 (+0.17); from the product to the four-row add 2.45 against 2.28 (+0.17); from there to the PSUM add 1.50 against 1.28 (+0.22, in which a semaphore increment is included). The reasoning was that most of the arithmetic can be done before the operation that it waits for ends. It can't here: behind each `ch(...)` it begins only after that operation's end, in all steps, so all of it shows. "Nothing shows this arithmetic" was wrong too, the view of one line of the kernel before shows it:

```profile
L2514 DVEq FUSED_REGOPS  x128: 53/127/161, 3690.8 to 4932.6; - x128
```

The upper bound was too low because I took it from the gap between steps, which has no relation to the length of the new arithmetic. Only the mask's part is shown by a run, middle_unmasked's 69 us; the other 0.5 us a step are read from the rows, and no run isolates them.

**The exp wait: right.** The 1.84 us are not a longer wait. From the copy to the clearing of the exp's semaphore 1.58 us pass in the change and in blocks_bare_exp alike (medians); then the change computes the address of the buffer half for 0.17 us, and blocks_bare_exp goes on at 1.68. Together a later step came out at 9.88 where 8.96 was forecast with its registers, and 101 x 0.92 = 93 us of the 117 that the last attention is over its forecast.

**The slack: mis-sized.** I took back all 87 us that VectorE waited for gathers; 29.6 remain, 18.2 of them in front of the first step, so 57 were taken back. The forecast had -60 as an end of its range. That the slack exists and is spent once is shown by the two halves, 164 + 43 against 265.

**Waiting for TensorE at closings: over-sized.** 45 us forecast, 22.9 measured in 11 waits; one_product gives 16. The 3.7 us that eight records were to take at the lower level were 3.88. An opening step grew by 1.54 us up to its last operation (medians) where 1.28 was forecast with its registers, +6. Together 93 + 6 + 30 - 22 = 107 of the 117; the rest lies around the tiles.

**The gate's attention: wrong.** -35 forecast, -3.8 measured. Gathers were the bound and became fewer, but the bound didn't stay theirs: in [2500, 2600] POOL is 60% busy instead of 76. The mask's arithmetic is in these steps too (29.6 us of idle before it, 65 times), and 10.6 us went to SyncE's wait for surplus gathers at the end; that TensorE's turns (87% busy there in both) hold back the rest is argued, not shown. I had taken 32 gathers at their full price less 7, that is, I had the bound stay where it was.

**Building the tables: right.** +15 forecast, +16.4 measured. SyncE's queue and the first operation of the counting:

```profile
467.10 68.27 SPq L244 DMA_DIRECT2D table_main<-graphs_main_ell  x48
...
538.17 27.36 SPq L252 DMA_DIRECT2D table_main<-graphs_main_ell  x13
...
583.60 35.22 SPq L244 DMA_DIRECT2D table_gate<-graphs_five  x17
...
621.59 26.65 SPq L252 DMA_DIRECT2D table_gate<-graphs_five  x13
...
650.35 1.21 SPq L349 DMA_DIRECT2D table_gate<-graphs_empty  x2
...
654.76 0.23 DVE L1352 CAST count_iota_b<-iota 128x128 bf16<-128x128 f32 x1 [27.94 <-PEq L62]
```

The closing octets are 13 in 27.36 us, 2.2 apart (2.3 forecast), main closed at 565.5 (575), gate at 648.2 (647), padded at 651.6 (652), and VectorE's last placing, at 626.8 now, no longer ends the stage.

**The rivals.** Gathers as the bound (1) is refuted by POOL's 350 us of waiting. Exp without its table load (2): 112 of the 126 had one. Hidden after all (3): the reverse. TensorE late inside tiles (4): one_product refutes it for the change; in late_row_add, where its sums were wanted sooner, it came true. The drain (5): the exp begins at 4705.68, where the load of 4704.38 ends, and VectorE goes on 0.30 us after the exp's end. The Trainium skill ("ScalarE: Activation LUTs", "What ACT_TABLE_LOAD costs") has a drain of 1.38 us with every switch to a different set; by that a step would take about 11.3 us, an estimate, and the trace with its 9.88 does not agree. This load follows an earlier exp; a real switch shows no drain either: in the kernel before the exp of 4601.44 ends at 4601.67, the load for the gelu begins at 4601.69 and the gelu at 4602.99.

## What to carry to other kernels

Before work is taken off an engine, ask what waits it was covering. Of four adds of 3.14 us the wait for another engine's answer covered 1.6, so taking them off can save only the rest; with nothing taken off and the order alone changed, the cover was worth 96 us. Sharing octets between tiles saves gathers but adds steps, and where the engine that pays per step is next to the bound, 14 steps of 8 us weigh more than 64 gathers of 1.3. In a chain in which each operation waits for the end of the one before, register arithmetic between two operations was not hidden in any step: count it at its full length, and keep it out of the loop's middle where only the ends need it. And ask of a last round what its surplus work holds up.

## What the runs showed of the hardware

TensorE ran the sums mostly at the lower of its two levels. Eight records of 264 columns took 3.88 us after some 6 us of idleness, at a granted clock of 0.50 (1.2 GHz, 4711.6 to 4715.5), and 1.94 us directly behind the experts' products, at 1.00 (2.4 GHz, in late_row_add at 4700.54). Of the change's 126 sums 98 took over 3.5 us, 15 under 2.2, and 13 lay between. Short bursts between pauses should be priced at the lower level, and so a product that "hides" needs twice the room.

In one comparison the kernel before took 5404 to 5447 us in 24 runs, 7% more than beside all other kernels. The three kernels beside it were slower than in their second runs too, but not alike: by 406 us (blocks_empty_row), 211 (late_one_product) and 251 (stream_own_unmasked). So not even their order can be used there. In the trace of blocks_empty_row ten of ScalarE's 99 table loads in the last attention begin 7 us or more behind VectorE's signal; in that of its second run none begins later than 0.11. The cause is outside of what the profile shows and stays open, and only comparisons with the kernel before at its usual time were used.
